# A pipelined attention and int8 feed-forward kernel: the max pass half a phase further ahead, one shift chain per batch

## The reference

```python
qkv = x @ attn_w.T + attn_b                       # 16 heads, 3 x 8 channels each
scores = where(mask, k . q / sqrt(8), -10000)     # key <= query
probs = softmax(scores, over keys)
x = layernorm(x + (probs . v) @ out_w.T + out_b)
q_lhs, q_rhs = round(x / row absmax * 127), round(rhs / column absmax * 127)
x = layernorm(x + (q_lhs @ q_rhs) * both scales)
```

## Time and profile before

| what | value |
|---|---|
| median of 3 runs | 286.72 us |
| range of the runs | 286.15 to 288.01 us |
| span of the profiled execution, first to last instruction | 285.2 us |
| what lies around the span, median less span | 1.5 us |
| busy share of the span: PE, DVE, ACT, POOL | 84%, 79%, 66%, 38% |
| mean granted TensorE clock | 0.974 of full |

### The profile page before, as it was taken

The page is one execution under the profiler, slowest core; times in us unless marked ns, Lnnn a source line. Parts: engine busy times, 40 slices in busy tenths (PEclk is TensorE's granted clock), DMA queues, the critical chain, the costliest instruction groups (busy, mean ns, idle before and its releaser), DMA issues.

```text
span 285.2 us, 9729 instructions
## 1 busy us (share of the span) xinstructions
PE 239.1 (84%) x3259; PEld 173.3 (61%) x3259; DVE 226.7 (79%) x658; ACT 187.6 (66%) x434; POOL 109.6 (38%) x216
## 2 busy tenths in 40 slices
PE   2469798999898998979898979898998989898520
PEld 1326566777676776757676757676776767665310
DVE  7618878788888889798989898888889798984431
ACT  3121475777678596859687777779595867677641
POOL 7730304060717162424334261617162523242542
PEclk9999999999999999999999999999999999999955
DMA  3396292828182735455564728282736445101001
GB/s 92 125 224 116 80 203 77 190 85 180 59 196 89 172 107 151 77 161 98 162 116 140 138 86 192 74 200 79 165 75 173 84 156 87 38 8 37 18 18 37
DMA packets 50905, 32.54 MB, mean 114 GB/s; under 512 B 7260, under 2 KB 50876, under 8 KB 50876
## 3 DMA queue, kind: packets, MB, share of 16 engines
q1 hardware_dynamic: 50876, 32.18, 46.0%
HBM read 17.17 MB, written 14.68 MB: 112 GB/s over the span
## 4 chain that ended last, share of the span: by engine, by line
PE 48%; DVE 22%; DMA 11%; issue 10%; SPq 3%; ACT 2%; POOL 1%; DVEq 1%; ACTq 0%; POOLq 0%
PE pv_bank L861 11%; PE max_bank L817 10%; DMA k_stat<-imagek 7%; DVE part_max L644 7%; PE exp_bank L817 7%; DVE shift L680 5%; PE bank_b L897 4%; PE max_bank L820 3%; PE exp_bank L820 3%; PE bank_a L949 3%; DVE ffn L742 3%; PE bank_b L929 2%; DMA imagek<-qk_parts 2%; DVE shift L677 2%; PE bank_a L941 2%
## 5 line engine op out<-in xcount | busy, mean ns | idle before, releaser
L490 ACT ACTIVATE probs<-exp_bank 128x512 f32<-128x512 f32 (+1 forms) x192 | 101.3, 531 | 61.8 <-PE exp_bank L820 60.7
L644 DVE TRANSPOSE_TENSOR_REDUCE part_max<-max_bank 128x16 f32<-128x512 f32 (+1 forms) x192 | 116.9, 617 | 20.2 <-PE max_bank L820 18.8
L817 PE MATMUL max_bank<-q_move,k_stat 124*128 124x128 bf16 (+3 forms) x512 | 70.2, 239 | 20.6 <-DVE part_max L644 16.0
L817 PE MATMUL exp_bank<-q_move,k_stat 128*128 128x128 bf16 (+3 forms) x512 | 66.9, 233 | 0.7 <-DMA q_move<-shift 0.7
L817 PEld LDWEIGHTS max_bank<-q_move,k_stat 124*128 124x128 bf16 x512 | 39.7, 117 | 42.0 <-DVE part_max L644 21.4
L861 PE MATMUL pv_bank<-probs,v_stat 128*32 128x256 f32 (+3 forms) x1024 | 61.1, 311 | 0.0
L820 PE MATMUL max_bank<-causal,identb 128*128 128x128 bf16 (+1 forms) x192 | 46.0, 240 | 0.0
L820 PE MATMUL exp_bank<-causal,identb 128*128 128x128 bf16 (+1 forms) x192 | 45.5, 237 | 0.0
L430 POOL TENSOR_TENSOR qk_rest<-qk_f,qk_parts 128x512 f32<-128x512 f32 x15 | 17.4, 1163 | 72.5 <-ACT qk_f L506 72.5
L817 PEld LDWEIGHTS exp_bank<-q_move,k_stat 128*128 128x128 bf16 x512 | 42.0, 114 | 2.6 <-DMA q_move<-shift 1.2
L452 POOL TENSOR_SCALAR rstd<-moments 128x2 f32<-128x2 f32 x32 | 6.1, 191 | 78.3 <-DVE moments L757 69.1
(11 more groups left out here) (84 smaller groups left out, 332.8 us busy)
## 6 DMA issues: line engine op xcount, KB each, us to landing
imageq<-qk_parts SPq DMA_DIRECT2D x32, 192.0 KB, 1.9
imagek<-qk_parts SPq DMA_DIRECT2D x32, 192.0 KB, 2.0
q_move<-imageq SPq DMA_DIRECT2D x32, 192.0 KB, 4.1
k_stat<-imagek SPq DMA_DIRECT2D x32, 192.0 KB, 4.4
xt_in<-xt_dram SPq DMA_DIRECT2D x16, 128.0 KB, 2.2
x_in<-x_dram SPq DMA_DIRECT2D x16, 128.0 KB, 2.4
out_dram<-o SPq DMA_DIRECT2D x16, 128.0 KB, 1.9
q_move<-shift SPq DMA_DIRECT2D x32, 8.0 KB
```

Source lines behind the costliest of these rows:

```text
L490: act.activation(probs[u][:, 0:cols], exp_bank[u % EXP_BANKS][:, 0:cols], ACT.Exp, scale=SCALE).then_inc(exp_done[1], 1)
L644: dve.tensor_reduce(o32, max_bank[u % MAX_BANKS][:, 0:n * (TOK - key)].rearrange("k (c q) -> k c q", q=32), op=ALU.max, axis=AX.X, apply_t ...
L817: pe.matmul(tiles[:, j, :], keys, q_move[b.ring][0:rows, p0 + j, key:TOK], start=(j == 0), stop=False, skip_group_check=True)
```

## The change

- The max pass runs one and a half phases ahead of the exponentials, where it ran one ahead: in slots 0 to 5 of phase b PE and DVE do units 6 to 11 of batch b+1, in slots 6 to 11 units 0 to 5 of batch b+2.
- The shift is made once per batch, for all eight pairs: one `join_maxima` in slot 6, one `turn_maxima` of 2 products (before, 4 for each group) in PE's slot 7, and `make_shift` in three DVE instructions in slots 7 and 8. The negated maximum stays in PSUM (`bank_b`, columns 64 to 96); one cast and one subtraction read it there. `load_shift` is two DMAs of two rows each, behind one another, where it was one DMA of four rows for each group.
- Other new slots: on PE `project_qk(b+3)` in 0 (was 8) and `turn_zq` in 11; on ACT `qk_from_psum(b+3)` in 1 and 2 (was 8 and 9), `pv_from_psum` in 3, `norm1` in 4, `v_from_psum` in 5, `norm2` in 6 (was 11), `round_z` in 9; on DVE `second_part(b+3)` in 6 (was `second_part(b+2)` in 0), `second_stats` in 3 and 4, `normalise` in 5, `first_sum` in 9 to 11; on POOL and SP a new order of the list.
- q and k operands, their DRAM images and xt have rings of four. `load_ones` is 16 DMAs of one row, where it was 6 of two rows, and 8 of them stand ahead of SP's first image write, 8 ahead of its second batch.
- All phases are written out; there is no loop.

```diff
+def max_unit(b, u):
+    return (b + 1, u + HALF) if u < HALF else (b + 2, u - HALF)
...
@@ SP @@
             def phase(b):
-                write_image(b + 2, 0)
-                load_shift(b, 1)
-                write_image(b + 2, 1)
                 load_xt(b + 4)
                 load_x(b)
-                read_image(b + 2)
-                load_shift(b + 1, 0)
+                write_image(b + 3, 0)
                 store(b - 3)
+                write_image(b + 3, 1)
+                load_shift(b + 1)
+                read_image(b + 3)
...
+            def load_shift(b):
+                if not real(b):
+                    return
+                wait(sp, shift_made, b)
+                wait(sp, exp_scores, b - QK_RING)
+                for part in range(2):
+                    row = SHIFT_ROW + 2 * part
+                    sp.dma_start(q_move[b % QK_RING][row:row + 2, :, :].rearrange("s p (c q) -> s (p c) q", q=32),
+                                 shift[:, part, :]).then_inc(shift_loaded, 16)
...
             def last_rows_stand():
                 sp.wait_ge(pool_setup, POOL_FIRST)
-                load_ones((RING - 1,))
+                load_ones(range(2, QK_RING))
...
                 for i in slots:
                     for s in range(2):
-                        row = SHIFT_ROW + 2 * s
-                        sp.dma_start(k_stat[i][row:row + 2, :, s, :],
-                                     ones_b[:, :].unsqueeze(1).to_broadcast([2, PAIRS, TOK])).then_inc(ones_loaded, 16)
+                        for row in (SHIFT_ROW + s, SHIFT_ROW + 2 + s):
+                            sp.dma_start(k_stat[i][row:row + 1, :, s, :],
+                                         ones_b[0:1, :].unsqueeze(1).to_broadcast([1, PAIRS, TOK])).then_inc(ones_loaded, 16)
...
@@ POOL @@
             def phase(b):
-                split(b + 2, True)
                 add_residual(b - 3)
+                split(b + 3, False)
+                norm_factors(b - 3, 1, r_stats, rstd2_made)
+                split(b + 3, True)
                 add_bias(b - 1)
-                norm_factors(b - 3, 1, r_stats, rstd2_made)
-                split(b + 3, False)
                 norm_factors(b - 1, 0, y_made, rstd_made)
...
+            def make_shift(b, step):
+                if step == 0:
+                    wait(dve, max_turned, b)
+                    dve.tensor_reduce(bank_b[:, 64:96], bank_b[:, 0:64].rearrange("c (w q) -> c q w", w=2),
+                                      op=ALU.max, axis=AX.X, negate=True).then_inc(shift_made[1], 1)
+                elif step == 1:
+                    wait(dve, shift_made, b, 1)
+                    if b > 0:
+                        dve.wait_ge(shift_loaded, 32 * b)
+                    dve.tensor_copy(shift[:, 0, :], bank_b[:, 64:96]).then_inc(shift_made[1], 1)
+                else:
+                    wait(dve, shift_made, b, 2)
+                    dve.tensor_tensor(shift[:, 1, :], bank_b[:, 64:96], shift[:, 0, :],
+                                      ALU.subtract).then_inc(shift_made[1], 1)
...
@@ DVE @@
             def phase(b):
                 for u in range(NU):
+                    if u == HALF:
+                        join_maxima(b + 1)
+                    maxima(*max_unit(b, u))
...
+                    if u == 6:
+                        scales(b - 2, 1)
+                        if b >= -1:
+                            second_part(b + 3)
+                    if u == 7:
+                        make_shift(b + 1, 0)
+                        scales(b - 2, 2)
+                        make_shift(b + 1, 1)
+                    if u == 8:
+                        make_shift(b + 1, 2)
...
@@ PE @@
             def turn_pv(b):
                 wait(pe, pv_out, b)
-                if (b + 1).real:
-                    wait(pe, shift_made, b + 1, 5)
+                if real(b + 4):
+                    wait(pe, qk_out, b + 4)
```

More of the change, by code:

```diff
@@ L75, with real, phases @@
 MAX_BANKS, EXP_BANKS = 2, 3
[L76 to L114, removed]
+def real(b):
+    return 0 <= b < NBATCH
+def phases(phase, before={}):
+    for b in range(-3, NBATCH + 3):
         if b in before:
             before[b]()
[L117 to L122, removed]
+        phase(b)
+def max_unit(b, u):
+    return (b + 1, u + HALF) if u < HALF else (b + 2, u - HALF)
 def build_program(nc, x, xt, wqkv_t, bqkv, wo_t, bo, rhs_t, out):
@@ L261, in build_program, with wait, wait_ring @@
         o_made = signal("o_made", 2)
[L263 to L282, removed]
+        def wait(eng, sig, b, n=None):
+            if real(b):
+                eng.wait_ge(sig[1], per[sig[0]] * b + (per[sig[0]] if n is None else n))
+        def wait_ring(eng, sems, b, each, n=1):
+            if real(b):
+                eng.wait_ge(sems[b % len(sems)], 16 * (each * (b // len(sems)) + n))
         def tiles_of(bank, u):
@@ L303, in _ @@
             sp.dma_start(rhst[:, :], rhs_t).then_inc(rhs_in, 16)
+            sp.dma_start(xt_in[1][:, :], xt[1]).then_inc(xt_loaded[1], 16)
             def load_xt(b):
-                if not b.real or (b.turn is None and b.base == 0):
+                if not real(b) or b < 2:
                     return
-                wait(sp, v_proj, b - RING)
-                sp.dma_start(xt_in[b.ring][:, :], xt[b.number()]).then_inc(xt_loaded[b.ring], 16)
+                wait(sp, v_proj, b - XT_RING)
+                sp.dma_start(xt_in[b % XT_RING][:, :], xt[b]).then_inc(xt_loaded[b % XT_RING], 16)
@@ L330, in read_image @@
             def read_image(b):
-                if not b.real:
+                if not real(b):
                     return
-                wait_ring(sp, image_written, b, 4, 4, apart=True)
-                wait(sp, exp_scores, b - RING)
+                wait_ring(sp, image_written, b, 4, 4)
+                wait(sp, exp_scores, b - QK_RING)
+                slot = b % QK_RING
                 for s in range(2):
                     rows = slice(s * ROWS, (s + 1) * ROWS)
[L337 to L340, removed]
@@ L342, in load_shift @@
-            def load_shift(b, g):
-                if not b.real:
-                    return
[L345 to L348, removed]
+                    q = image[0][slot].rearrange("(p s i) r q -> s (i r) p q", s=2, i=HD)
+                    k = image[1][slot].rearrange("(p s i) r q -> s (i r) p q", s=2, i=HD)
@@ L410, in _ @@
                                         base=0, pattern=[[-1, KB]], channel_multiplier=1))
-            for i in range(1, RING):
+            for i in range(1, QK_RING):
                 step(pool.memset(q_move[i][:, :, :].bitcast(F32), 0.0))
-            step(pool.memset(k_stat[2][:, :, :, :].bitcast(F32), 0.0))
+            for i in range(2, QK_RING):
+                step(pool.memset(k_stat[i][:, :, :, :].bitcast(F32), 0.0))
             assert done[0] == POOL_FIRST, done[0]
@@ L424, in split @@
             def split(b, last):
-                if not b.real or (b.turn is None and b.base == 0):
+                if not real(b) or b == 0:
                     return
@@ L446, in norm_factors @@
             def norm_factors(b, n, have, made):
-                if not b.real:
+                if not real(b):
                     return
                 t, m = rstd[n], moments[n]
-                wait(pool, have, b, apart=True)
+                wait(pool, have, b)
                 pool.tensor_scalar(t[:, 0, :], m[:, :, 1], EPS, 1.0, ALU.add, ALU.mult).then_inc(made[1], 1)
@@ L456, in norm_factors @@
                 pool.tensor_tensor(t[:, 1, :], m[:, :, 0], t[:, 0, :], ALU.mult).then_inc(made[1], 1)
-                wait(pool, made, b, 3, apart=True)
+                wait(pool, made, b, 3)
                 pool.tensor_scalar(t[:, 1, :], t[:, 1, :], -1.0, 0.0, ALU.mult, ALU.add).then_inc(made[1], 1)
             def add_residual(b):
-                if not b.real:
+                if not real(b):
                     return
@@ L805, in _ @@
             set_up()
-            phases(dve, phase)
+            phases(phase)
         @block.tensor
```

306 lines of the change are left out of this document (139 added, 167 removed).

## The result

The changed kernel takes 300.88 us (median of 5 runs, 300.56 to 302.37) against 286.72 (286.15 to 288.14) for the kernel before, run on the same chip: a ratio of 1.0485, 95% interval 1.0451 to 1.0518. It is slower by 4.9%, and above my range of 277 to 295. Its profiled execution, the slowest of the five (302.37), has a span of 300.7 us, 15.5 more than before, and a granted clock of 0.962 on the mean, against 0.974.

The account below looks back on a forecast made before the run. PE was taken as close to the bound, waiting 1.23 us per phase for DVE. Start +7.5, phases -1.4, +1.4, -2.6, -3.0, -1.0 gave +0.9 on 285.2: span 286.1, with 1.5 around it 287.6 us, range 277 to 295.

Parts of the forecast that it names:

- Step 1: Shift chain on DVE and PE: slow subtractions go, one join of 0.5, cast and subtraction 0.2 each, PE's 1.23 wait saved.
- PE alone would then need 13.7 us: Steady phase: PE's 15.20 us less the 1.23 wait for DVE and 0.3 saved on turning the maxima.
- the forecast wait of 0.7: PE's slot 4: turn_pv, ready at about 5.5, waits for ACT's copy of pv_bank until 6.2, some 0.7 us.
- my 14.4 for PE's own path: Steady phase on PE's own path, with the 0.7 us wait in slot 4 included: 14.4 us.
- Step 2: Steady phase laid out through PE, ACT, DVE, POOL and SP: shift rows land at 15.1, so 15.2 us per phase, as before.
- The store of 0.4 fits in POOL's split: SP's list in the steady phase: the 0.4 us store adds nothing before the second image half, whose issues end at 12.5.
- Step 4: Sum over start, phases and drain against the span of 285.2: +0.9, span 286.1, with the drain taken as untouched.
- Step 3: The start: one-row loads of ones delay batch 1's image to 32.0; exp scores of batch 0 at 38.5, 7.5 us later.
- The chain is longer: Rival, 0.24: shift DMAs queue behind two image writes; landing 2.4 after issue gives 293 us, 2.8 gives 299.
- The shift rows are in time: Rival, 0.20: SP reaches load_shift 0.8 us earlier or rows land sooner; phase 14.4, total 277.3 us.
- PE alone sets the phase: Rival, 0.06: ACT's copy isn't late either; 13.7 us per phase, about 270 us.
- The change doesn't do what it says: Rival: the subtraction from PSUM still waits for POOL, 0.3 us per phase, +4 us; its chance counted inside the 0.24 rival.

Follow-up runs that it names:

- shift first: The changed kernel with SP issuing the two shift-row DMAs ahead of the second half of the image write: 295.41 us, ratio 1.0256 to the kernel before.
- ones later: The changed kernel with SP's second eight loads of ones behind batch 1's image instead of ahead of it: 300.21 us, ratio 1.0435 to the kernel before.
- the written-out kernel: The kernel before with its shift chain in PSUM and all phases written out, no loop: 278.55 us, ratio 0.9700 to the kernel before.
- `norm2` late in the drain: The changed kernel with norm2 back in ACT's slot 11 from phase 16 on: 298.73 us, ratio 1.0390 to the kernel before.
- shift first, pv transposes later: The changed kernel with shift-row DMAs ahead of the second image half and turn_pv behind the scores of slot 5 instead of slot 4: 292.10 us, ratio 1.0166.
- the combinations with the ones later: Three changed kernels with shift rows earlier, norm2 late and second ones loads later: these edits 288.72 us; plus turn_pv later 286.53; plus store behind image read 284.02.
- these three together: The changed kernel with shift rows ahead of the second image half, norm2 late in the drain and second ones loads after batch 1's image: 288.72 us, ratio 1.0059.
- before, shift in PSUM: The kernel before with only the shift chain kept in PSUM, PE's waits on bank_b moved to match: 276.37 us, ratio 0.9617 to the kernel before.

## Why the prediction was wrong

The median is 13.3 us above the forecast 287.6; the spans, of the profiled execution, differ by 300.7 - 286.1 = 14.6 us. By the forecast's terms: start +1.9 (40.4 against 38.5), phases 0 to 2 +1.0 (12.3, 15.1, 15.3 against 12.0, 14.6, 15.05), phases 3 to 12 +6.3 (15.83 against 15.2), 13 and 14 +1.3, phase 15 +0.3, drain +3.5. That makes 14.3. The other 0.3 is a slip in my sum: I took the start from exp scores to exp scores, but the phases of the kernel before from max scores, which begin 0.3 earlier in phase 0 and are missing in phase 15.

**Step 1 was right for DVE, and too low for PE.** Cast and subtraction took 0.19 and 0.15 us (0.2 each), the join 0.60 (0.5), and the wait for DVE is gone. The PSUM form is free of POOL, and alone it is worth 11.5 us. But "PE alone would then need 13.7 us" was 0.5 short. With the forecast wait of 0.7 in it, my 14.4 for PE's own path measured 14.97 in "shift first", and no version here has a steady phase below 14.2. The 1.23 us that I took off were the wait of one phase; over the run the waits were 16.0 us in 16, 1.0 each on the mean. The rest of the 0.5 stays open.

**Step 2 was right in mechanism; its sum is the term that was mis-sized.** "15.2 us per phase, as before" measured 15.83. In the phase at 162.53 the lateness builds up by tenths. The copy `heads_t` ended at 6.45 (6.2), since slot 1 began at 1.9 (1.7), and `second_part` was done at 10.65 (10.3). The split ended at 174.42, at 11.9 (11.5). "The store of 0.4 fits in POOL's split" cost another 0.1: SP had first to issue both DMAs of the first half, which become ready with the same DVE instruction as the split, and the store ended at 174.50. The first shift DMA went out at 13.1 (12.5), the second at 13.7 (13.1), and the landing took 2.04 (2.02). So no step by itself was off by more than 0.2 us, and 0.4 of the 0.6 was there when POOL's split ended. A sum of nine steps whose sign hangs on 0.15 us could not carry the forecast. "Every 0.1 us on the path costs 1.4" gives +8.8 for the 0.63. "Shift first" confirms the mechanism by taking the shift rows' place in the list away.

**Step 4, "The drain is untouched", is the step that failed outright.** I weighed `norm2` in slot 6 by the steady phase, where its factors are ready 0.7 us before. In the drain, the phases are short and nothing stands between POOL's factors and their use, so ACT's order decides: +3.5, of which the mend gave back 3.1.

**Step 3 was 1.9 us short.** Batch 1's image landed at 33.74; I had 32.0. The eight one-row loads began at 17.02 (16.2) and took 5.40 (5.2), the last read was issued at 28.17 (26.9), and its transfer took 5.57 (5.08). From the landing to the exp scores it was 6.63 us, where I had 6.5. So the halved clock from 35.2 to 38.6, which I had named and put no price on, explains little of the late start: this part of the sum leaves 0.1 us for it. With the ones later, the scores began 3.0 us earlier, and there the clock did cost, 1.4 us.

**The other rivals.** "The chain is longer" had 0.24, and the sign and size are its own, but not its mechanism: it had the rows land 2.4 to 2.8 us after issue, and they landed after 2.04. "The shift rows are in time" is what "shift first" makes; the four image waits there are what I had missed. "PE alone sets the phase" came true nowhere in the new order. "The change doesn't do what it says" is refuted by L641: 153 ns is its median over the batches, 192 the longest.

**What stays open**: why some image writes hold SP's queue for 0.7 to 1.9 us where others take 0.43; the 0.9 us by which phase 14 is longer than forecast; what PE's phase of 14.2 us consists of beyond the forecast 13.7; and what makes the written-out kernel 3.1 us longer, its image waits included.

## What to carry to other kernels

When a reordering brings several gains at once, take the change apart: here one line of it (an intermediate kept in PSUM, so that DVE has only one SBUF operand beside a busy GpSimd) is worth 4%, and the new order around it, with the loop written out, costs 9%, of which writing out is some 1% if it costs here what it cost in the order of before. Lay out the queue of the engine that issues DMAs as strictly as PE's, each issue 0.35 to 0.55 us in its own place, and let the transfer that someone waits for go first. Check a moved step in the drain and at the start as well as in the steady phase, and put a price on each clock drop that you name. When the sign of a forecast hangs on a tenth of a microsecond in a sum of nine steps, say that the sign is open.

## What the runs showed of the hardware

The granted clock of PE fell at the start, to the 1.2 GHz level, for some 3.4 us after PE had been busy for 0.42 of 4 us (the kernel after, 30 to 34), and in the written-out one after 0.32 of 2 us (18 to 20). In the kernel before, the same stretch, 18 to 20, has 0.63 us of work and keeps 1.00; but it keeps 1.00 too after 10 to 12 with 0.14 us of work, so what decides is not shown here. Four products of 256 columns in fp32 took 1.08 us at the higher level and 2.02 at the lower. The fall is there too in "shift first", "`norm2` late in the drain", "ones later" and "shift first, pv transposes later", and not in the combinations with the ones later. What it costs depends on what PE has to do then: in "ones later" it met batch 0's phase, which took 13.75 us in place of 12.3; in "`norm2` late in the drain" the clock was low in three stretches from 32 to 38 and part of the next, twice as long as in the kernel after, and the first exp scores still began 0.6 us earlier than there, with the wait for batch 1's image 0.9 us shorter.

SP's issue of one image write took 0.43 us in most phases; the longest was 0.84 in the kernel after, 1.22 in the one before and 1.95 in "these three together", with the same shape; a two-row shift DMA took 0.52 to 0.60, and a one-row load of 4 KB 0.63 (0.68 from one to the next), more than the image write that is 48 times as large.

A cast with its one operand in SBUF took 0.74 us at the longest beside POOL's work, and the same cast from PSUM 0.18 (L677, the kernel before and "before, shift in PSUM").
